# Attention and mixture-of-experts layer: expert and x transfers at other times, projection weights in two parts, another order in the prologue

## The reference, cut to what matters

```
x = x + attention(layernorm(x))      # 16 heads of 64, bias by relative position
x = x + experts(layernorm(x))        # 16 experts, each token goes to its best 4

attention: q, k, v = h @ Wq, h @ Wk, h @ Wv            # 128 -> 16 x 64
           scores = q k^T + rel_bias[bucket(mem - ctx)]
           out = softmax(scores) v, heads joined, @ Wo # 1024 -> 128
experts:   logits = -|h - keys|^2 + h rw^T + rb; top 4; w = softmax(top 4)
           out = sum of w * (gelu(h w1^T + b1) w2^T + b2)   # 128 -> 512 -> 128
```

## Time and profile before

| | |
|---|---|
| times of three runs | 1163.38, 1163.86, 1169.29 us (median 1163.86) |
| profiled execution | 1169.13 us |
| its span | 1167.3 us |
| mean granted clock of TensorE | 0.964 of full speed |
| busy: PE, DVE, ACT, POOL | 1073.4, 863.9, 885.8, 719.9 us |
| attention phase | to about 830 us |
| expert phase | about 835 to 1125 us |
| sum over the experts and output | about 1130 to 1167 us |

### The profile page before, as it was taken

How to read it: one execution, slowest core, us unless ns; L and a number is a source line. 1 busy time by engine, 2 the same in 40 slices (tenths; PEclk the granted TensorE clock), 3 DMA queues, 4 the chain that set the end, 5 groups by cost and what they waited for, 6 DMA issues and landing times. The chain is left out here.

```text
span 1167.3 us, 27501 instructions
## 1 busy us (share of the span) xinstructions
PE 1073.4 (92%) x8436; PEld 858.9 (74%) x8437; DVE 863.9 (74%) x2507; ACT 885.8 (76%) x2111; POOL 719.9 (62%) x887
## 2 busy tenths in 40 slices
PE   5997999999999999999999999798699999999940
PEld 2675777777777777777777777575599999999940
DVE  5776799889889889988988988687366444444439
ACT  4786888888888888888888888686376667676745
POOL 2443455674675676567467566547257776767657
PEclk9899999999999999999999999899699999999985
DMA  6775566676676666667667667878433232222137
GB/s 186 213 213 167 158 170 184 179 199 181 174 199 170 192 188 183 182 181 198 177 173 203 170 188 200 298 219 260 125 120 101 88 84 80 75 68 64 46 91 270
DMA packets 138113, 193.18 MB, mean 165 GB/s; under 512 B 19215, under 2 KB 110871, under 8 KB 137992
## 3 DMA queue, kind: packets, MB, share of 16 engines
q1 hardware_dynamic: 128840, 174.83, 53.0%
q0 software_dynamic: 9152, 16.88, 4.5%
HBM read 103.26 MB, written 90.33 MB: 166 GB/s over the span
## 5 line engine op out<-in xcount | busy, mean ns | idle before, releaser
L549 POOL TENSOR_SCALAR shared<-shared,rinv 128x512 f32<-128x512 f32 x512 | 349.2, 693 | 289.3 <-DVE rinv L701 287.6
L595 ACT ACTIVATE shared<-shared,nmax 128x512 f32<-128x512 f32 x512 | 365.9, 716 | 115.6 <-DVE nmax L695 110.5
L695 DVE CUSTOM_DVE_ANT_0 shared<-bank,shared 128x512 f32<-128x512 f32 x512 | 334.0, 680 | 16.3 <-PE bank L859 14.1
L1175 POOL DMA_INDIRECT y_dram<-yb,home x158 | 179.7, 1137 | 85.2 <-issue 59.2
L711 DVE STREAM_TRANSPOSE turned<-shared 128x512 f32<-128x512 f32 x256 | 166.8, 689 | 15.4 <-issue 12.2
L875 PE MATMUL bank<-idn,shared 128*128 128x128 f32 x1024 | 151.6, 281 | 9.1 <-POOL shared L549 7.3
L314 POOL DMA_INDIRECT xs_dram<-copies,slot x128 | 135.5, 1058 | 33.8 <-issue 20.2
L1384 PE MATMUL bank<-shared,act_h 128*128 x1264 | 155.0, 276 | 1.2 <-DVE yb L1311 0.7
L875 PEld LDWEIGHTS bank<-idn,shared 128*128 128x128 f32 x1024 | 118.4, 143 | 44.5 <-POOL shared L549 23.2
L1384 PEld LDWEIGHTS bank<-shared,act_h 128*128 128x128 f32 x1264 | 149.2, 193 | 1.6 <-issue 1.6
L601 ACT ACTIVATE pt_e<-bank 128x512 f32<-128x512 f32 x256 | 144.5, 591 | 6.2 <-PE bank L875 6.1
(11 more groups left out here) (153 smaller groups left out, 1938.7 us busy)
## 6 DMA issues: line engine op xcount, KB each, us to landing
pt_dram<-turned SPq DMA_DIRECT2D x512, 128.0 KB
pt_d<-pt_dram SPq DMA_DIRECT2D x128, 512.0 KB, 4.4
xb<-xs_dram SPq DMA_DIRECT2D x79, 129.0 KB
shared<-in_experts SPq DMA_DIRECT2D x16, 514.0 KB, 6.0
shared<-y_dram SPq DMA_DIRECT2D x32, 256.0 KB, 6.6
shared<-roll_dram SPq DMA_DIRECT2D x4, 768.0 KB, 7.5
y_dram<-yb,home POOLq DMA_INDIRECT x158
xs_dram<-pad_sb SPq DMA_DIRECT2D x17, 129.0 KB, 2.8
```

Source lines behind the costliest of these rows:

```text
L549: pool.tensor_scalar(tile, tile, rinv[:, 2 * v + hh:2 * v + hh + 1], 1.0, ALU.mult, ALU.mult)\
L595: act.activation(prob[:, v, hh, :], prob[:, v, hh, :], ACT.Exp, bias=nmax[:, n:n + 1], scale=-1.0, accum_out=rsum[:, n:n + 1]).then_inc(ex ...
L695: dve.tensor_tensor_reduce(prob[:, v, hh, :], score_bank(v, hh)[:], strips[:, 2 * i + hh, v * P:v * P + S], -1.0, BIG, ALU.add, ALU.min, n ...
L1175: pool.indirect_dma_start(y_dram, bass.IndirectOffsetOnAxis(ap=home[:, j, c:c + 1], axis=0), yb[:, j, c, :], None, bounds_check=TOP * T - ...
```

## The change

- SyncE issues the first x ahead of the prologue's small tables. The three projection weights are issued by ACT, ahead of everything else that it does. The identity has a semaphore of its own (ld_i), on which PE waits after the matmuls of the bias.
- The projection weights are split in two parts of columns: FIRST (256 columns, pairs 0 and 1) in the prologue, OTHERS (768 columns) of k in the prologue too, those of q and v on ACT after the first queries, on VectorE in extras (0, 0). PE waits for them at step (0, 1).
- ACT's prologue has another order: the copies of the bias first, then far bias and its strip, then weights and tokens. VectorE copies its far strip ahead of `normalise`.
- The routing constants, the wait for x of batch 1 and the moments of batch 1 go from extras (0, 0) to late_extras (0, 0). The wait for all later x goes from extras (0, 7) to extras (1, 0). POOL waits for ld_r in the first routing "copy".
- `load_expert` is called once at the end of steps (1, 0) to (1, 3), for experts 0 to 3, which fit below AHEAD; in the last batch at most twice per step, under the same limit of columns.

```diff
--- before.py
+++ after.py
@@ -186,7 +186,7 @@
         ps_s, ps_t, ps_a, ps_o = banks[0:4], banks[4:6], banks[6], banks[7]
 
 
-        ld_x0, ld_x1, ld_x, ld_c, ld_w = sem("ld_x0"), sem("ld_x1"), sem("ld_x"), sem("ld_c"), [sem(f"ld_w{n}") for n in "kqv"]
+        ld_x0, ld_x1, ld_x, ld_c, ld_i, ld_w = sem("ld_x0"), sem("ld_x1"), sem("ld_x"), sem("ld_c"), sem("ld_i"), [sem(f"ld_w{n}") for n in "kqv"]
         ld_wo, roll_st, ld_strip = sem("ld_wo"), sem("roll_st"), [sem(f"ld_strip{g}") for g in range(H // TC)]
         ld_r, one_rdy, bf_rdy = sem("ld_r"), sem("one_rdy"), sem("bf_rdy")
         w_hi_rdy, w_lo_rdy = sem("w_hi_rdy"), sem("w_lo_rdy")
@@ -213,6 +213,8 @@
             "pick_rdy", "mask_rdy", "rank_rdy", "free_rdy", "carry_rdy", "sel_rdy", "slotf_rdy", "slot_rdy"))
         copy_rdy, sent = sem("copy_rdy"), [sem("sent_even"), sem("sent_odd")]
         ld_ex, tab, at_rdy = sem("ld_ex"), sem("tab"), sem("at_rdy")
+
+        FIRST, OTHERS = slice(0, VW), slice(VW, H * DH)
 
         def far_strips(a, first, end):
 
@@ -294,6 +296,8 @@
                 pool.wait_ge(ve2, n + 1)
                 pool.tensor_tensor(rstd[:, 1], var_eps[:, 1], minus_half[:], ALU.pow).then_inc(rstd2, 1)
             elif stage_no == "copy":
+                if n == 0:
+                    pool.wait_ge(ld_r, LD_R)
                 pool.wait_ge(xn2, (n + 1) * TC)
                 pool.nop(nofuse=True)
                 pool.tensor_copy(copies[:, :, 1, 0:D], copies[:, :, 0, 0:D]).then_inc(copy_rdy, 1)
@@ -462,12 +466,10 @@
 
         @block.sync
         def _(sp):
+            sp.dma_start(x_all[:, 0:TC, :], x[0:S].rearrange("(n p) d -> p n d", p=P)).then_inc(ld_x0, 16)
             sp.dma_start(rb_sb[:], rel_bias).then_inc(ld_c, 16)
             sp.dma_start(onehot_sb, onehot.rearrange("n (a m) -> n a m", a=2)).then_inc(ld_c, 16)
-            sp.dma_start(x_all[:, 0:TC, :], x[0:S].rearrange("(n p) d -> p n d", p=P)).then_inc(ld_x0, 16)
-            sp.dma_start(idn[:], ident).then_inc(ld_c, 16)
-            for n, w in enumerate((wk, wq, wv)):
-                sp.dma_start(stage[n], w).then_inc(ld_w[n], 16)
+            sp.dma_start(idn[:], ident).then_inc(ld_i, 16)
 
             sp.wait_ge(roll_cp, 2)
             sp.dma_start(roll_dram.rearrange("h (a m) -> h a m", a=2), roll_sb).then_inc(roll_st, 16)
@@ -510,7 +512,10 @@
                     sp.dma_start(pt_d[:, v].rearrange("p a j h r -> p (a j h r)"),
                                  pt_dram[n % 2, v].rearrange("p a e -> p (a e)")).then_inc(pt_rd[v], 16)
 
-            free_to = [AHEAD + 2 * STRIP * (i + 1) for i in range(NPR)]
+            def free_to(b, i):
+
+                return AHEAD if b < LAST else AHEAD + 2 * STRIP * (i + 1)
+
             loaded = [0]
 
             def step(b, i):
@@ -521,7 +526,8 @@
                                  x[n * S:(n + 1) * S].rearrange("(n p) d -> p n d", p=P)).then_inc(ld_x, 16)
                 if b == LAST:
                     sp.wait_ge(neg_rdy, LAST * CHUNKS + (i + 1) * TILES)
-                    while loaded[0] < NE and (loaded[0] + 1) * EW <= free_to[i]:
+                for _ in range(2 if b == LAST else 1 if b == 1 else 0):
+                    if loaded[0] < NE and (loaded[0] + 1) * EW <= free_to(b, i):
                         load_expert(loaded[0])
                         loaded[0] += 1
 
@@ -564,7 +570,6 @@
             pool.wait_ge(far_cp, 1)
             for a in range(2):
                 pool.tensor_copy(far_strips(a, H // 2, H), far_bias(a, H // 2, H)).then_inc(far_late, 1)
-            pool.wait_ge(ld_r, LD_R)
             run_steps(step, lambda: None)
 
         @block.scalar
@@ -644,23 +649,30 @@
                         weights_t(LAST, NPR - 1, v, hh)
                 context(LAST, NPR - 1)
 
-            def weights_hi(n):
-                act.wait_ge(ld_w[n], 16)
-                act.activation(w_hi[n], stage[n], ACT.Copy).then_inc(w_hi_rdy, 1)
-
-            weights_hi(0)
-            weights_hi(1)
-            act.wait_ge(far_mm, 1)
-            act.activation(far_sb, ps_t[0][:, 0:2 * H].rearrange("p (a h) -> p a h", a=2), ACT.Copy).then_inc(far_cp, 1)
-            tokens_hi(0)
+            def weights_hi(n, cols):
+                act.activation(w_hi[n][:, cols], stage[n][:, cols], ACT.Copy).then_inc(w_hi_rdy, 1)
+
+            for n, w in enumerate((wk, wq, wv)):
+                act.dma_start(stage[n], w).then_inc(ld_w[n], 16)
             for a in range(2):
                 act.wait_ge(roll_mm, a + 1)
                 act.activation(roll_sb[:, a, :], ps_s[a][0:H, :], ACT.Copy).then_inc(roll_cp, 1)
-            weights_hi(2)
+            act.wait_ge(far_mm, 1)
+            act.activation(far_sb, ps_t[0][:, 0:2 * H].rearrange("p (a h) -> p a h", a=2), ACT.Copy).then_inc(far_cp, 1)
             act.wait_ge(far_cp, 1)
             act.activation(far_strips(0, 0, H // 2), far_bias(0, 0, H // 2), ACT.Copy).then_inc(far_rdy, 1)
+            act.wait_ge(ld_w[0], 16)
+            weights_hi(0, FIRST)
+            tokens_hi(0)
+            act.wait_ge(ld_w[1], 16)
+            weights_hi(1, FIRST)
+            act.wait_ge(ld_w[2], 16)
+            weights_hi(2, FIRST)
+            weights_hi(0, OTHERS)
             keys_hi(0, 0, ps_s[2])
             queries_hi(0, 0, ps_o)
+            weights_hi(1, OTHERS)
+            weights_hi(2, OTHERS)
             run_steps(step, drain)
 
         @block.vector
@@ -731,16 +743,20 @@
                     dve.wait_ge(kk_rdy, 1)
                     dve.tensor_tensor(lconst[:], lrow[:], ps_t[1][:, 0:NE], ALU.subtract).then_inc(lc_rdy, 1)
 
+            def weights_lo(n, cols, order):
+                dve.wait_ge(w_hi_rdy, order)
+                dve.tensor_tensor(w_lo[n][:, cols], stage[n][:, cols], w_hi[n][:, cols].bitcast(F32), ALU.subtract)\
+                    .then_inc(w_lo_rdy, 1)
+
             def extras(b, i):
 
-                if b == 0:
-                    if i == 0:
-                        routing_constants(0)
-                        dve.wait_ge(ld_x1, 16)
-                    if i == NPR - 1:
+                if (b, i) == (0, 0):
+                    weights_lo(1, OTHERS, 5)
+                    weights_lo(2, OTHERS, 6)
+                if b < LAST:
+                    if (b, i) == (1, 0):
                         dve.wait_ge(ld_x, 16 * (NB - 2))
-                if b < LAST:
-                    if i == 0:
+                    if i == 0 and b:
                         for stage_no in range(3):
                             moments_of(dve, b + 1, 0, stage_no, st_rdy, mv_rdy, ve_rdy)
                     if i == 6:
@@ -753,6 +769,11 @@
 
             def late_extras(b, i):
 
+                if (b, i) == (0, 0):
+                    routing_constants(0)
+                    dve.wait_ge(ld_x1, 16)
+                    for stage_no in range(3):
+                        moments_of(dve, 1, 0, stage_no, st_rdy, mv_rdy, ve_rdy)
                 if (b, i) == (0, 1):
                     routing_constants(1)
                 if exists(b - 1):
@@ -792,19 +813,17 @@
             dve.wait_ge(ld_x0, 16)
             for stage_no in range(3):
                 moments_of(dve, 0, 0, stage_no, st_rdy, mv_rdy, ve_rdy)
+            dve.wait_ge(far_cp, 1)
+            dve.tensor_copy(far_strips(1, 0, H // 2), far_bias(1, 0, H // 2)).then_inc(far_rdy, 1)
             normalise(dve, 0, 0, xn, rstd_rdy, xn_rdy)
-            def weights_lo(n):
-                dve.wait_ge(w_hi_rdy, n + 1)
-                dve.tensor_tensor(w_lo[n], stage[n], w_hi[n].bitcast(F32), ALU.subtract).then_inc(w_lo_rdy, 1)
-
-            weights_lo(0)
+
+            weights_lo(0, FIRST, 1)
             tokens_lo(0)
-            weights_lo(1)
+            weights_lo(1, FIRST, 2)
+            weights_lo(2, FIRST, 3)
+            weights_lo(0, OTHERS, 4)
             keys_lo(0, 0, ps_s[2])
             queries_lo(0, 0, ps_o)
-            dve.wait_ge(far_cp, 1)
-            dve.tensor_copy(far_strips(1, 0, H // 2), far_bias(1, 0, H // 2)).then_inc(far_rdy, 1)
-            weights_lo(2)
             dve.wait_ge(far_rdy, 2)
             run_steps(step, drain)
 
@@ -947,6 +966,8 @@
                 if n == 0:
                     pe.wait_ge(w_lo_rdy, 3)
                     project_v(0, ps_t[1])
+                if n == 1:
+                    pe.wait_ge(w_lo_rdy, 6)
                 if n == 2:
                     pe.wait_ge(ld_wo, 16)
                 if exists(two[0]):
@@ -985,7 +1006,7 @@
                 weigh(LAST, NPR - 1)
                 project_out(LAST, NPR - 1)
 
-            pe.wait_ge(ld_c, 48)
+            pe.wait_ge(ld_c, 32)
             for a in range(2):
                 pe.matmul(ps_s[a][0:H, :], rb_sb[:], onehot_sb[:, a, :], start=True, stop=True).then_inc(roll_mm, 1)
 
@@ -993,6 +1014,7 @@
                 mm = pe.matmul(ps_t[0][:, a * H:(a + 1) * H], onehot_sb[:, a, m:m + 1].broadcast_to([NBUCKET, P]), rb_sb[:],
                                start=True, stop=True)
             mm.then_inc(far_mm, 1)
```

(1 more changed line is left out.)

## The result

The changed kernel took 1159.54 us (median of seven runs, 1155.99 to 1162.21), the one before beside it on the same chip 1165.85 (seven runs, 1163.38 to 1169.29): a ratio of 0.9947, with the interval 0.9926 to 0.9968. It is faster by 6.3 us; I had forecast 17.0 and the time 1147. The profiled execution took 1159.45 us, its span is 1157.6, the mean granted clock 0.974.

What follows compares the result with a forecast made beforehand. PE was taken as the bound outside a few holes. First hole 8.0, second hole 8.7 and prologue 0.3 us sum to 17.0, off the median of 1163.86: 1147 us, range 1141 to 1157.

Steps and rivals of the forecast that it cites:

- the prologue's term: Prologue, up to the last reciprocal of step (0, 0): gain 0.3 us, bounds a gain of 2.5 and a loss of 6.
- rival 3: Prologue: DMA queues take turns, so the one-hot table lands late; 6 us lost, time 1153.2 with the full loss; chance 0.06.
- my path: Prologue chain from far_sb through VectorE's strip copy, normalise (1.11), transposes and tokens: first projection at 14.7 us, first score 19.9.
- The second hole's second part: Interval after the one behind step (7, 0): 13.95 against 12.62 us, an excess of 1.33 that the change would remove.
- The main part: Interval behind step (7, 0), where five experts delay pt_d: 19.06 against 11.73 us, an excess of 7.33 to be removed.
- The first hole: Step (0, 7), at 107.5 us: VectorE and PE wait for x; moving the wait to (1, 0) gains 8.0 us.
- rival 4: Step (0, 7): another chain is late there, and 4 of the 8 us stay; time 1151; chance 0.06.
- The experts in batch 1: Steps (1, 0) to (1, 3): four moved experts cost 0 there, at most 6.9 us.
- Rival 1: Batch 1: DMA time is conserved, so the moved experts cost 6.9 us there; time 1153.8; chance 0.12.
- rival 5: Steps (1, 1) to (1, 4): experts delay pt_d reads, PE idles, its clock falls; 34.6 us lost, 1181.5; chance 0.03.
- Profile or median: Profiled execution 5.3 us above the median: placed in the expert phase, so 1147 from the median, not 1152.1, was forecast.
- rival 2: The profile's extra 5.3 us sat in the two holes, so the median had less to win: 1152.1; chance 0.12.

Runs made afterwards that it cites:

- experiment 3: The changed kernel with the three projection weights issued by SyncE again, behind the identity, not by ACT: 1156.59 us, ratio 0.9898.
- experiment 7: The changed kernel with rel_bias and the one-hot table issued ahead of x on SyncE, weights still on ACT: 1158.08 us, ratio 0.993.
- Experiment 4: The changed kernel with POOL's two far-strip copies made to wait until after VectorE's normalise: 1157.57 us, ratio 0.9919.
- experiment 5: The changed kernel with the weights on SyncE's queue again and VectorE's far-strip copy behind queries_lo: 1152.84 us, ratio 0.9902.
- Experiment 6: The changed kernel with only VectorE's far-strip copy put back behind queries_lo, weights still on ACT: 1156.16 us, ratio 0.9912.
- experiments 8: The changed kernel with SyncE's order rel_bias, one-hot table, x, identity, weights, and VectorE's far-strip copy behind queries_lo: 1154.43 us, ratio 0.9891.
- experiment 9: Experiments 8's kernel with routing constants, batch 1's x wait and moments at step (0, 2), POOL's far copies behind the other far strips: ratio 0.9872.
- experiments 1: The kernel before with only the wait for later x at (1, 0) and experts 0 to 3 in batch 1: 1152.97 us, ratio 0.9882.
- experiment 2: The kernel before with only the wait for later x moved to (1, 0): 1157.13 us, ratio 0.9909.
- 12: The kernel before with only experts 0 to 3 moved into batch 1: 1186.64 us, ratio 0.9963.
- 11: The kernel before with the moves of experiments 1, repeated on another chip: 1179.02 us, ratio 0.9893.

## Why the prediction was wrong

**The step that failed is the prologue's term**, "Gain 0.3 us": 8.0 us were lost at the first ctxt copy, 7.5 after the next, and one of the forecast's own signs of being wrong, a first matmul after 6 us, came (8.16). Two of its numbers were wrong by some 3 us each; the chain between them was right.

- "Some 0.5 us of delay" for the one-hot table on shared queues was 3.3 (6.3 us from issue to landing instead of 2.4). Experiments 3 and 7 show it. I had counted on equal turns, twice 386 KB at about 200 GB/s. They were not equal in bytes. The queues of the kernel after up to 8.07 us, when the table landed (packets, MB, share of the engines; q10 is ACT's, q1 SyncE's):

```profile
q10 hardware_dynamic: 409, 1.54, 52.2%
q1 hardware_dynamic: 702, 0.44, 19.6%
```

  ACT's queue had moved nearly all of the weights, at 3.8 KB a packet, SyncE's less than a third as much, at 0.6 KB. This is rival 3, which had 0.06: the table came with the last of all 1.9 MB. It cost half of that rival's 6 us because the engines moved 310 GB/s from 1.7 to 8.07 us and not 200. The rule that the prediction cited from the Trainium skill (DMA: Bandwidth & Descriptors, Queues, rings and completion order), turns packet by packet, agrees with these rows; I had read it as turns of equal bytes.
- "Normalise 1.11" was read from a stretch where POOL stood still. The change puts POOL's two copies, released by the same far_cp, beside it, and it took 4.26: 3.15 us that none of my rivals named. Experiment 4 shows it (1.11 us once POOL waits), and 5 and 6 have 1.11 too. The Trainium skill, SBUF — State Buffer (section Who interferes with whom), says that VectorE and GpSimd share a pair of ports, and that this is an exclusive lock: whoever issues first holds it for the whole instruction, and the other is blocked. By it a copy or tensor_scalar in its two-port mode contends for them, and an operation with two inputs in SBUF contends with a GpSimd instruction that reads SBUF. The rows agree, 1.91 and 0.33 us for the same operation here, 1.79 and 0.43 for the subtraction in experiments 8 and 9.
- The order itself, far_sb and VectorE's far copy ahead of normalise, was in my path, and it holds: 14.7 + 3.0 (far_sb at 12.75 instead of 9.75) + 3.15 = 20.8, and the first projection was at 21.03. Experiment 6 shows what this order, with the lock, cost: 2.8 us at the first score, 4.5 at the first copy.
- From the first projection to the first score it took 6.25 us and not 5.2. PE's first three products of queries and keys took 1.65 us (25.46 to 27.11), where they had taken 0.97 (16.71 to 17.68), the last of them 0.66 us against 0.43: about 0.7 of the 1.1 us. These are durations as at the lower clock level (0.63 at 39.99 us, where the granted clock reads 0.50), after a wait of 5.82 us for xt, though the granted clock reads 1.00 here; the last section comes back to this.
- Behind the first score the forecast won another 0.7 us (0.4 late there, 0.3 early at the end), which did not come: from the first score to the first copy it is 25.59 us, and was 25.40. ACT waits 1.68 us for the first scores of step (0, 1), where it had waited 0.89: they stand behind the routing constants and moments that the change put at the end of step (0, 0). In experiment 9, which moves these on, the wait is 0.89 again.

**The second hole's second part** (1.33 of 8.66) did not come: 14.01 us after, and 13.6 to 14.4 in experiments 1, 2 and 12. Before, PE was busy through this interval, with 4 matmuls more than after, so the excess there was work that the hole had pushed into it (read from the busy times); that is gone. A new wait has taken its place, that of POOL ahead of rstd (1.92 us). In the twelve kernels without the burst this interval grows with that wait, 13.17 us with 1.07 (experiment 7), 13.61 with 1.51 (12), 14.12 with 2.02 (5), and the one less the other is 11.8 to 12.1 in all. By its code this operation waits until the scatters of the last routing have landed, but the profile names no releaser. One batch earlier the wait is 0.19 us, and there no experts are loaded. So I suspect the two that step (7, 1) issues in every version (736.69 and 737.64 us in the kernel after): they may make the scatters land late. No kernel left them out, so this is only argued. The main part was 7.1 for 7.33.

**The first hole** was right: 8.06 for 8.0, and rival 4 (another chain late at (0, 7)) falls with the 12.56 us of experiment 2.

**The experts in batch 1** cost nothing in experiments 1, 7 and 11 and 0.2 to 1.0 us in the other kernels that have the move, summed over the eight intervals from the copy behind (0, 7) on: 96.86 us before, 97.38 in the kernel after, 97.48 in 12, at most 97.82 (experiment 3). Rival 1, that they pay the burst's price of 6.9, falls, and rival 5 with it.

**Profile or median:** the 5.3 us between them I placed in the expert phase. Of them 2.0 were in the median of three runs: that of seven is 1165.85 us. Where the other 3.3 sat is not shown. The 337.9 us behind the last copy do not mark the expert phase, since 6 and 7 have 337.9 and 338.8 there; the burst's 2.5 us less in experiment 2 speak for rival 2 in part, in one trace against one.

Of the 10.7 us between the forecast gain (17.0) and the measured (6.3), 8.3 are the prologue's, less 0.5 in the interval behind it, 1.6 the second hole's, 0.5 batch 1's and 0.35 the last interval's but one. What is left, 0.5, is within the intervals, but it holds two larger things that nearly cancel: the two traces differ behind the last copy by 3.1 us in favour of the kernel after, and in span by 9.7 us where the medians differ by 6.3. The chance of 0.93 for faster came out; the range, down to 1141 and up to 1157, ended 2.5 us short, since its upper end took each loss of the prologue as a mishap by itself and not as two on one chain.

Open are the cost in batch 1, there in some versions and not in others, POOL's wait in the last batch, and why one chip takes 25 us longer in the expert phase.

## What to carry to other kernels

When an operation is moved, price it by what will run beside it, not by its old row: see which other engine is released by the same semaphore, and whether the two share a port. In a prologue follow the smallest transfer that all wait for; large ones on another queue delay it, even if they were issued to save time. And test the parts of a change apart: here two moves of transfers were worth 14 us and the third part took half of it back.

## What was unexpected of the hardware

- The lock works both ways and is long: four operations of 0.33 us took 3.15 us more beside two copies of 1.9 us. In the kernel before POOL's two copies took 4.72 us, beside VectorE's wq_lo subtraction (1.24 us), against 3.72 in experiment 5, unseen since nobody waited for POOL; that this is the same lock the other way is read from the rows and not tested.
- The clock's row and the durations disagree in the prologue. In the windows 20 to 25 and 30 to 35 us of the kernel after the granted clock is 1.00 in both, yet the same product (xnt_hi with wq_hi, 128x512) takes 0.63 us at 23.33 and 0.40 at 32.51. Where the row reads 0.50, at 39.56 and 39.99 us, products of 512 columns take 0.63 us as well. So I take the lower level for the time around 23 us; this is an inference from durations.
- Turns between two DMA queues were far from equal in bytes: 1.54 MB against 0.44 up to 8.07 us, the larger share going to the queue with the larger packets.
